# A gated attention and quantised feed-forward layer: sigmoid levels shared with GpSimd, weight block scales spread, extra products at two seams

## The reference

```python
def act_qdq(x):
    qmax = 2.0 ** (ACT_BITS - 1) - 1.0
    scale = jnp.maximum(jnp.max(jnp.abs(x)) / qmax, 1e-12)
    return jnp.clip(jnp.round(x / scale), -qmax - 1.0, qmax) * scale
def fixed_qdq_u16(x):
    scale = 1.0 / 65536.0
    return jnp.clip(jnp.round(x / scale), 0.0, 65535.0) * scale
...
x = x + jnp.tanh(g_xattn[0]) * _L0_xattn_ref(_layernorm(x), ctx_1024, ctx_1024, ...)
x = x + jnp.tanh(g_ffn[0]) * _L0_ffn_ref(_layernorm(x), w_gate, w_up, w_down)
...
x = act_qdq(x)                                   # inside _L0_ffn_ref
up = act_qdq(x @ lpbq_dequant(w_up).T)
gate = act_qdq(x @ lpbq_dequant(w_gate).T)
sig = fixed_qdq_u16(jax.nn.sigmoid(gate))
gate = act_qdq(gate * sig)
o = act_qdq(gate * up)
return o @ lpbq_dequant(w_down).T
```

## Time and profile before

| what | value |
|---|---|
| median of 3 runs | 616.76 us (614.8 to 617.37) |
| the profiled execution | 616.58 us, span 614.7 us |
| mean granted TensorE clock | 0.981 |
| PE busy | 564.1 us (92% of the span) |
| DVE busy | 493.8 us (80%) |
| ACT busy | 439.0 us (71%) |
| POOL busy | 207.5 us (34%) |
| chain that ended last, by engine | PE 22%, ACT 12%, DVE 7%, issue 4% |

### The profile page before, as it was taken

The page is one execution under the profiler, slowest core; times in us unless marked ns, Lnnn a source line. Parts: engine busy times, 40 slices in busy tenths (PEclk is TensorE's granted clock), DMA queues, the critical chain, the costliest instruction groups (busy, mean ns, idle before and its releaser), DMA issues. The chain is left out here.

```text
span 614.7 us, 11698 instructions
## 1 busy us (share of the span) xinstructions
PE 564.1 (92%) x4315; PEld 339.9 (55%) x4315; DVE 493.8 (80%) x835; ACT 439.0 (71%) x632; POOL 207.5 (34%) x227
## 2 busy tenths in 40 slices
PE   2679999899999999999987899999999899949998
PEld 1345666566665666666445444444444344438887
DVE  5788889999999988998828599979988799954442
ACT  2237888678787777887766354549999998869860
POOL 4723347766666879755345000000000000010100
PEclk9889999999999999999999799999999999969999
DMA  6523344455544444433241000000000000023443
GB/s 192 133 87 116 102 127 130 120 144 134 144 132 138 125 132 127 119 81 106 66 116 53 2 1 1 0 1 1 1 1 0 1 0 1 1 69 104 138 138 103
DMA packets 42812, 48.98 MB, mean 80 GB/s; under 512 B 10436, under 2 KB 30532, under 8 KB 42756
## 3 DMA queue, kind: packets, MB, share of 16 engines
q1 hardware_dynamic: 40916, 43.38, 24.2%
q0 software_dynamic: 1408, 4.46, 2.6%
q10 hardware_dynamic: 432, 0.39, 0.3%
HBM read 24.32 MB, written 8.70 MB: 54 GB/s over the span
## 5 line engine op out<-in xcount | busy, mean ns | idle before, releaser
L872 DVE TENSOR_REDUCE negm<-s_ps 128x2 f32<-128x512 f32 x256 | 163.5, 682 | 25.2 <-PE s_ps L516 24.5
L695 ACT ACTIVATE pt<-st_ps 128x512 f32<-128x512 f32 x256 | 138.9, 596 | 54.8 <-PE st_ps L531 53.8
L1205 PE MATMUL pairs<-xq,wut 128*128 128x512 f16 x576 | 124.7, 379 | 2.7 <-ACT lnall L1357 1.6
L1205 PEld LDWEIGHTS pairs<-xq,wut 128*128 128x128 f16 x576 | 56.2, 98 | 71.1 <-issue 2.3
L516 PE MATMUL s_ps<-kst,qst 96*128 96x256 f16 x512 | 81.0, 274 | 11.0 <-DVE negm L872 7.6
L531 PE MATMUL st_ps<-qst,kst 97*128 97x512 f16 x256 | 76.5, 379 | 1.5 <-DMA qst<-mrow 0.9
L455 PE MATMUL pv_ps<-pt,vt 128*32 128x256 f32 x1024 | 68.5, 385 | 0.6 <-ACT pt L695 0.6
L1645 POOL PARTITION_ALL_REDUCE vmax<-vmax x5 | 1.8, 357 | 194.8 <-DVE vmax L1464 119.8
L516 PEld LDWEIGHTS s_ps<-kst,qst 96*128 96x128 f16 x512 | 46.0, 98 | 33.3 <-DVE negm L872 23.1
L1205 PE MATMUL pairs<-xq,wgt 128*128 128x512 f16 x276 | 60.5, 379 | 0.0
L1280 PE MATMUL pairs<-wdt,h 128*128 128x256 f16 x384 | 49.4, 281 | 8.4 <-ACT h L1393 8.4
(11 more groups left out here) (207 smaller groups left out, 1047.4 us busy)
## 6 DMA issues: line engine op xcount, KB each, us to landing
qst<-qk SPq DMA_DIRECT2D x96, 64.0 KB, 2.1
kst<-qk SPq DMA_DIRECT2D x45, 128.0 KB, 3.2
xt<-in_x SPq DMA_DIRECT2D x16, 256.0 KB, 4.3
ct<-in_ctx SPq DMA_DIRECT2D x16, 256.0 KB, 2.9
xr<-in_x SPq DMA_DIRECT2D x16, 256.0 KB, 3.9
out<-y SPq DMA_DIRECT2D x16, 256.0 KB, 3.8
lnall<-out POOLq DMA_DIRECT2D x8, 512.0 KB, 4.3
recb<-rec_dram SPq DMA_DIRECT2D x15, 256.0 KB
```

The lines of the kernel that those rows point to most:

```text
L695: nc.scalar.activation(pt[:, (j // 2) % 2, j % 2, kt], st_ps[u % 3][:], ACT.Exp, scale=1.0 / (WS * WS * HD ** 0.5)).then_inc(exp_done, 1)
L872: nc.vector.tensor_reduce(negm[:, b % 2, tt, lo:lo + 5:4], s_ps[tt][:], AX.X, ALU.max, negate=True).then_inc(max_done, 1)
L1205: mm = nc.tensor.matmul(ps[:, p, k, :], w[:, a, dt, f * P:(f + 1) * P], xq[:, b, c, dt, :], start=n == 0, stop=n == len(terms) - 1)
```

## The change

- POOL computes the sigmoid levels of two of three tiles in chunks 0 to 6 and of one in chunk 7: gb times 65536 plus 2^23, then minus 2^23 and at most 65535, both f32 and in place. ACT keeps the others. `gated` reads these levels from `gb` as f32 instead of `ib`. The reduction for the largest gate value now comes on POOL behind the levels of chunk 0, and the other three behind all levels.
- `SCALES` holds six steps for each weight: three reductions, scaling, reciprocal, step of the blocks. The clipping comes one step later.
- PE gets 6 products of 128x512 at the end of attention, and 32 before the down products. Nothing reads their results.

```diff
--- before.py
+++ after.py
@@ -24,6 +24,7 @@
 QMAX = 32767.0
 BLOCK = 32
 LEVELS = 65536.0
+WHOLE = 8388608.0
 
 
 def attention(nc, t, x, ctx, out):
@@ -45,7 +46,7 @@
     LAST = NB - 1
     END = PAIRS * NB
     WEIGHTS = ("w_gate", "w_up", "w_down")
-    SCALES = (2, 34, 66)
+    SCALES = ((-3, -2, 5, 5, 6, 6), (21, 22, 29, 30, 37, 38), (54, 61, 62, 69, 70, 71))
     PARTS = 3
 
     xv = x.rearrange("b (p t) d -> b p t d", t=KT)
@@ -621,6 +622,9 @@
                 turn_weights(2, k)
             pe.wait_ge(ltop_done, 1)
             nc.tensor.matmul(pv_ps[:, 1, 0:1], row1[:], ltop[:], start=True, stop=True).then_inc(ltop_spread, 1)
+            for _ in range(6):
+                nc.tensor.matmul(s_ps[0][:].rearrange("p a b -> p (a b)"), wo2[:, 0, 0, 0:P],
+                                 wo2[:, 0].rearrange("p a b -> p (a b)"), start=True, stop=True)
 
         @block.scalar
         def _(act):
@@ -763,12 +767,19 @@
                 nc.vector.tensor_reduce(bm[:, n0:n0 + NBLK // PARTS], blocks(wt[i][:, at0:at0 + WP]), AX.X, ALU.max,
                                         apply_absolute_value=True).then_inc(blk_max, 1)
 
-            def block_scales(i):
+            def scale_of_blocks(i):
                 dve.wait_ge(blk_max, PARTS * (i + 1))
+                if i:
+                    dve.wait_ge(blk_scaled, 2 * i)
                 nc.vector.tensor_scalar(bs[:], bm[:], 1.0 / 7.0, 1e-12, ALU.mult, ALU.max).then_inc(blk_scaled, 1)
+
+            def inverse_of_blocks(i):
                 dve.wait_ge(blk_scaled, 2 * i + 1)
                 dve.wait_ge(w_divided, PARTS * i)
                 nc.vector.reciprocal(bi[:], bs[:]).then_inc(blk_inv, 1)
+
+            def step_of_blocks(i):
+                dve.wait_ge(blk_scaled, 2 * i + 1)
                 dve.wait_ge(w_real, PARTS * i)
                 nc.vector.tensor_scalar(bf[:], bs[:], FS, None, ALU.mult).then_inc(blk_scaled, 1)
 
@@ -950,14 +961,17 @@
                     dve.wait_ge(wo_high, 1)
                     nc.vector.scalar_tensor_tensor(out=wol, in0=wof[:], scalar=WS, in1=woh, op0=ALU.mult,
                                                    op1=ALU.subtract).then_inc(wo_low, 1)
-                for i, at0 in enumerate(SCALES):
-                    if at0 - 1 - g in (16, 8, 0):
-                        part_scales(i, 2 - (at0 - 1 - g) // 8)
-                    if g == at0 - 1:
-                        if i:
-                            dve.wait_ge(blk_scaled, 2 * i)
-                        block_scales(i)
-                for i, n in pieces_behind(g, 4):
+                for i, steps in enumerate(SCALES):
+                    for p in range(PARTS):
+                        if g == steps[p]:
+                            part_scales(i, p)
+                    if g == steps[3]:
+                        scale_of_blocks(i)
+                    if g == steps[4]:
+                        inverse_of_blocks(i)
+                    if g == steps[5]:
+                        step_of_blocks(i)
+                for i, n in pieces_behind(g, 5):
                     if n // PARTS == 0:
                         at0 = n % PARTS * WP
                         dve.wait_ge(w_rounded, PARTS * i + n + 1)
@@ -1135,6 +1149,8 @@
         p2_done = sem("f_p2_done")
         warmed = sem("f_warmed")
         units_set = sem("f_units_set")
+        sums_done = sem("f_sums_done")
+        levels_done = sem("f_levels_done")
         q3_first = sem("f_q3_first")
         h3_first = sem("f_h3_first")
         l3_first = sem("f_l3_first")
@@ -1169,6 +1185,13 @@
         def ahead(c, k):
             return c + k < NC
 
+        def level_tiles(c):
+
+            return 1 if ahead(c, 1) else PR - 1
+
+        def sq_before(c):
+            return sum(level_tiles(k) for k in range(c))
+
         last_half = ps[:, 0, 0, 0:D]
         first_turned = (ps[:, 3, 0], ps[:, 2, 0])
 
@@ -1205,6 +1228,11 @@
                         mm = nc.tensor.matmul(ps[:, p, k, :], w[:, a, dt, f * P:(f + 1) * P],
                                               xq[:, b, c, dt, :], start=n == 0, stop=n == len(terms) - 1)
                 return mm
+
+            def spare_products(bank, n):
+
+                for _ in range(n):
+                    nc.tensor.matmul(bank, wgt[:, 0, 0, 0:P], wgt[:, 0, 0, 0:CW], start=True, stop=True)
 
             first_turn()
 
@@ -1254,6 +1282,7 @@
                     pe.wait_ge(qu_done, PR * c + p + 1)
                     products(wut, c, p).then_inc(u2_done, 1)
             chunks(0, NC - 1, up_again)
+            spare_products(ps[:, 3, 1], 32)
 
             def down(c, d):
                 for b in range(CB):
@@ -1335,8 +1364,8 @@
                     act.wait_ge(g_late, PR)
                 nc.scalar.activation(gb[:, c], ia[:, d], ACT.Sigmoid, scale=col(SG)).then_inc(sig_done, 1)
                 act.wait_ge(sig_done, c + 1)
-                for p in range(1 if ahead(c, 1) else PR):
-                    part = slice(0, FT) if ahead(c, 1) else slice(2 * p, 2 * p + 2)
+                for p in range(level_tiles(c)):
+                    part = slice(2 * p, 2 * p + 2)
                     nc.scalar.activation(ib[:, d, part].bitcast(U16), gb[:, c, part], ACT.Copy, scale=LEVELS
                                          ).then_inc(sq_done, 1)
                 if ahead(c, 1):
@@ -1527,12 +1556,21 @@
                                         apply_absolute_value=True).then_inc(u_max, 1)
 
             def gated(c, d, p):
+                own = p < level_tiles(c)
+                if own:
+                    dve.wait_ge(sq_done, sq_before(c) + p + 1)
+                else:
+                    dve.wait_ge(levels_done, PR * c - sq_before(c) + p - level_tiles(c) + 1)
+                level = ib[:, d, 2 * p:2 * p + 2].bitcast(U16) if own else gb[:, c, 2 * p:2 * p + 2]
+                tile(c, d, p, level)
+
+            def tile(c, d, p, level):
 
 
 
                 nc.vector.tensor_tensor_reduce(gb[:, c, 2 * p:2 * p + 2].rearrange("p f w -> p (f w)"),
                                                ia[:, d, 2 * p:2 * p + 2].rearrange("p f w -> p (f w)"),
-                                               ib[:, d, 2 * p:2 * p + 2].bitcast(U16).rearrange("p f w -> p (f w)"),
+                                               level.rearrange("p f w -> p (f w)"),
                                                -1.0, 0.0, ALU.mult, ALU.max,
                                                cmax[:, 2, PR * c + p:PR * c + p + 1]).then_inc(p2_done, 1)
 
@@ -1547,15 +1585,12 @@
                     nc.vector.tensor_tensor(cmax[:, 2, PR * NC:PR * NC + 1], top_i[:], top_u[:], ALU.mult).then_inc(top_p2, 1)
                 for p in range(PR):
                     up_max(c, p)
-                    if p == 0:
-                        dve.wait_ge(sq_done, c)
                     gated(c - 1, (c - 1) % 2, p)
             dve.wait_ge(u_max, PR * NC + PR)
             whole(1, PR * NC)
             dve.wait_ge(all_max, 3)
             scale(vmax[:, 1, 1:2], UX, VX, SU, KU)
             for p in range(PR):
-                dve.wait_ge(sq_done, NC + p)
                 gated(NC - 1, (NC - 1) % 2, p)
             dve.wait_ge(p2_done, PR * NC + 2 * PR)
             dve.wait_ge(top_p2, 1)
@@ -1645,8 +1680,25 @@
                 nc.gpsimd.partition_all_reduce(vmax[:, i, 1:2], vmax[:, i, 0:1], P, RMAX).then_inc(all_max, 1)
 
             nc.gpsimd.partition_all_reduce(warm[:], t["lmaxall"][:], P, RMAX).then_inc(warmed, 1)
-            for n, i in enumerate((0, 4, 1, 2, 3)):
-                over_partitions(n, i)
+            over_partitions(0, 0)
+
+            def levels(c, p, n):
+
+                pool.wait_ge(sig_done, c + 1)
+                tile = gb[:, c, 2 * p:2 * p + 2]
+                nc.gpsimd.tensor_scalar(tile, tile, LEVELS, WHOLE, ALU.mult, ALU.add).then_inc(sums_done, 1)
+                pool.wait_ge(sums_done, n + 1)
+                nc.gpsimd.tensor_scalar(tile, tile, WHOLE, LEVELS - 1.0, ALU.subtract, ALU.min).then_inc(levels_done, 1)
+
+            n = 0
+            for c in range(NC):
+                if c == 1:
+                    over_partitions(1, 4)
+                for p in range(level_tiles(c), PR):
+                    levels(c, p, n)
+                    n += 1
+            for n, i in enumerate((1, 2, 3)):
+                over_partitions(n + 2, i)
 
             def body(c, d):
```

## The result

The changed kernel takes 659.66 us (median of 4 runs, 656.86 to 661.68) against 615.78 for the kernel before on the same chip (4 runs, 614.32 to 617.37). The ratio is 1.0709, with a 95% interval of 1.0658 to 1.0759: 44 us slower, where 613.4 was forecast and the range ended at 632. The profiled execution has a span of 655.0 us; it had 614.7 before.

The account below looks back on a forecast made before the run. ACT was taken to bound the up products' stage (8.5 us a chunk against PE's 7.8), and PE attention. 616.6 + 3.5 - 2.9 - 1.6 - 2.2 = 613.4 us; range 604 to 632.

Parts of the forecast that it names:

- the price of POOL's second operation: Up stage: each of POOL's 30 `tensor_scalar` of 128x1024 f32, first or second of a pair, taken as 1.1 us.
- The bracket: Limits for one POOL operation of 128x1024: 0.96 us from writing alone, 4.3 us from the 128x256 row.
- slow rival: Up stage: POOL is the bound above 1.9 us an operation; 631 us at 2.1 each, 697 at 4.3; chance 0.19.
- Part 1: Up stage: 15 level tiles move from ACT to POOL, with library changes on the path; +3.5 us.
- the rival of short changes: POOL's library changes take 2 us each instead of 5.9: -3.1 instead of +3.5, 606.8 us in all; chance 0.23.
- so it loses little: Start of chunk 1: its first POOL tile comes 5.5 us late, but PE may run two groups (5.2 us) ahead.
- The lock rival: Up stage: DVE's `gated` and POOL's operations block each other, 8.7 us a chunk; 622 us, chance 0.15.
- "Costs nothing" for the other wait: `top_integer` on ACT waits for POOL's second reduction, ready at about 431; over before ACT gets there, no cost.
- Part 2: Attention: block-scale operations spread over steps remove PE's pauses at 119.05 and 191.46; -2.9 us, bounds 0 and 3.
- Part 3: Seam between the two blocks: six unread products cost 0.8 us; -1.6 us if the clock holds, +0.8 if not.
- its fall: Seam: PE's clock falls despite the six products, 2.4 us more than forecast, 615.8 us; chance 0.07.
- Part 4: Before the down products: 32 unread products, hidden in PE's wait, keep the clock at full; -2.2 us, bounds 0 and 2.9.

Follow-up runs that it names:

- e5_mult_add: Changed kernel with POOL's second operation written as mult by 1 and add of -8388608, clamp at 65535 left out: 628.84 us, 1.0151 of the kernel before.
- e2_levels_alone: Kernel before with only POOL's levels added, none of the other changes: 664.48 us, 1.0754 of the kernel before.
- e9_no_six: Kernel before with the moved block scales and the 32 unread products, without the six at the seam: 612.29 us, 0.9900 of the kernel before.
- e10_no_32: Kernel before with the moved block scales and six unread products, without the 32 ahead of the down products: 615.43 us, 0.9949.
- e1_other_parts: Kernel before with the moved block scales and both sets of unread products, all levels staying on ACT: 611.98 us, 0.9918 of the kernel before.
- e4_subtract_add: Changed kernel with POOL's second operation written as subtract and add of 0, clamp at 65535 left out: 656.81 us, 1.0657 of the kernel before.

## Why the prediction was wrong

**The failed step is the price of POOL's second operation**, which the prediction itself called the weakest: "I take 1.1", for all 30. The bracket was right (0.96 to 4.3), and so was 1.1 for the first operation, which takes 1.04 by itself. The second took 3.67 by itself, and the mean over all 30 was 2.8 us: over the 1.9 from which the prediction's own slow rival has POOL as the bound. With the second operation alone changed to (mult, add), 31.2 of the up stage's 46.0 us went. The reason for the choice was wrong: the 128x256 row has two operands from SBUF and the pair (subtract, mult), and I made the operands the cause. The runs show the pair to be enough: with immediates alone, every pair tried but (mult, add) took 3.6 us or more. Whether such operands are slow as well, with a fast pair, no run shows, nor why some pairs are slow. The 128x2 row, by which I told the two apart, is too short to show a rate. What could have been seen in the trace: the two lines with 128x256 (L988 and L1027, both (subtract, mult)) were POOL's only `tensor_scalar` of real length, and their first operator is the one of the new second line.

The GPSIMD Engine Reference of the Trainium skill (section 3.1) has 1.03 cycles per element for bodies of up to two operators, an estimate of 0.9 us. The fast pair at 1.04 agrees roughly; the others, at 3.6 to 3.7, are at four times that, and the measurement decides.

**Part 1 otherwise.** Four library changes more, and 5.9 us each: 5.94, 6.92 and 5.96 in the rows above, so the rival of short changes falls; those ahead of a level are 1 to 2 us longer than assumed (6.92 here, 7.70 in e5_mult_add). The first is hidden behind ACT's sigmoid, as forecast. Part 1 was put at +3.5; alone it measured +47.5. The forecast had the up stage 5.0 longer. It became 46.0 longer, of which 31.2 hang on the form of the second operation. Of the other 14.8, 5.4 go with the last change, near the forecast's 5.0, and 8.0 with the pair in the middle, for which it had nearly nothing: "so it loses little", said of PE, was the second miss. These 8.0 hang on the lock too, since 9.4 of the 14.8 also go when the second operation goes. Even in e5_mult_add, chunk 1's first tile is ready 29.2 us after the gate reduction instead of the 26.0 worked out; PE, out of buffers, is busy 5.2 of the 10 us from 440 and sees its clock at 0.66; and the 0.7 a chunk of DVE's slack, by which the delay was to shrink, is taken by the lock.

**The lock rival** was right as a mechanism. At the forecast's price it was too large: 7.99 us a chunk in e5_mult_add in place of its 8.7. In the changed kernel it worked at another place, on POOL, which set the pace: a level tile took 5.87 us beside `gated` and 4.87 without it, which over twelve tiles is 12 us, an estimate from these rows. The first operations' mean of 1.87 instead of 1.04 is this. The section "Who interferes with whom" of SBUF — State Buffer in the Trainium skill has the one that comes first hold the port for its whole instruction. Beside the fast operations the rows agree; beside the slow one they do not, for `gated` at 452.56 began 0.07 us after POOL's of 452.49 (3.62 us long) and was held up by 0.8, not by 3.6.

**The slow rival** came nearest: at a mean of 2.8 us an operation 659.7 lies between its 631 (2.1 us) and 697 (4.3 us). I gave it 0.19, with most of it outside the range.

**"Costs nothing" for the other wait** was wrong by little: `top_integer` stood 2.2 us for POOL's reduction at 432.25, since the pair ahead of it was late.

**Part 2** was forecast at -2.9. The pauses of 1.41 us at 119.05 and of 1.12 at 191.46 are gone, and the changed kernel has a new one of 0.89 at 42.77. PE's waits for the maxima from 40 to 330 us come to 1.3 to 2.8 us in the 14 kernels with part 2, and to 4.7 before and 4.2 in e2_levels_alone, so some 2 us are gone there. By times, e9_no_six, parts 2 and 4 alone, is 5.35 us below before in its group (612.29 against 617.64); less the 2.1 of part 4 that leaves 3.2, of which up to 0.7 is its shorter stretch at the seam (73.4 against 74.1). So 2 to 3 us: right in its mechanism, and in size as far as the scatter lets one see.

**Part 3** was forecast at -1.6 if the clock held, and 0.07 given to its fall. It held in 4 of 13. The price of the products is right: from PE's last product of attention that is read to its first of the second block it is 3.29 us with them and 2.42 without (e9_no_six), so 0.87 against 0.8. The expectation that six would hold the clock, from one trace in which it fell just in that microsecond, was not. The term is -1.5 or +0.2 against the kernel before, and +0.2 is the likelier. In the changed kernel's profiled execution the clock happened to hold, and 1.5 of the 4.7 us by which its gate reduction came earlier are due to that.

**Part 4** was forecast at -2.2: 71.9 less 69.8 is 2.1, and 1.7 with e10_no_32 as the kernel without. Right, and its working (hidden products, clock at full) shows in the rows.

With part 2 at -2 to -3, part 3 at +0.2 and part 4 at -2.1, the three are -3.9 to -4.9 together, and e1_other_parts measured -5.0 (611.98 against 616.95).

## What to carry to other kernels

Before work goes to POOL, find a row with the same two operators and real length; when the only long row is slow, take it as the likely price until something excludes it, and do not explain it away by operands. Count the changes of program library that an order makes, 6 to 7.7 us each here, and keep them off the path by putting other engines' chunks ahead and behind. Move only as much as takes the old bound below the next engine (one tile of three here): the second tile bought nothing (an up stage of 63.4 us against 63.3), and it meets DVE more often. A delay in a pipeline lasts when the engine that takes it up has no slack, so price the delay and the slack together.

## What the runs showed of the hardware

- POOL's `tensor_scalar` with two immediates on 128x1024 f32: (mult, add) 1.04 us, to f32 or to uint16 alike; five other pairs 3.6 to 3.7 us (all without a `gated` beside them).
- A change of POOL's library is paid at each switch between reductions and these operations: 5.7 to 6.3 us towards the reduction (nine kernels), 6.9 to 7.7 away from it (the rows that end in "issue").
- DVE's operation with two inputs and a POOL operation shut each other out in both directions: 1.04 becomes 1.9 to 2.1 on POOL, 1.22 becomes 1.7 to 2.04 on DVE, according to which starts first. A slow POOL operation of 3.62 us holds DVE up by no more than a fast one (0.8 us), and where `gated` meets it in its course it grows itself by about that, from 3.67 to 4.48 (e4_subtract_add).
- Kernels with the same instructions up to this place find TensorE's clock there at 2.4 or at 1.2 GHz in different executions (first gate tile 2.75 or 4.4 us). With each of the two the time from the last product of attention to the gate reduction repeats within 0.1 us (72.6 or 74.3).
